# Masked attention joined to the shared-head attention three steps sooner

## Chip, cores, metric

One core of one Trainium2 chip. The metric is device microseconds for one execution of the whole program. The core has five engines with an instruction stream each: TensorE (PE; its weight loads are listed as PEld), VectorE (DVE), ScalarE (ACT), GpSimd (POOL) and SyncE (SP, which issues transfers only). Each works through its own stream in order, and they meet at semaphores.

## What is computed

Two decoder layers on x of shape (32, 128, 128): 32 batches of 128 tokens with 128 features. Layer 0 is self attention, cross attention and a mixture of experts, layer 1 is what the change touches:

```
x = x + L1_attn(layernorm(x))                  # "shared1": 16 heads of 64, averaged in groups of
                                               # four to 4 heads; scores + relative bias, softmax
x = x + L1_xattn(layernorm(x), ctx, ctx, mask) # "cross1": 16 heads of 8, keys and values from ctx,
                                               # energy = where(mask == 0, -1e10, q k / sqrt(8))
x = x + L1_ffn(layernorm(x))                   # mixture of 8 experts and a shared one
```

## The kernel before, in words

**Stages.** The program is written as two functions of engine streams, one after the other: `early` (both attentions and experts of layer 0) and `late` (layer 1). Every attention is a software pipeline. A step `k` on an engine emits the work of several batches at once, each at another point of its way; a batch is 128 tokens, a group is G = 2 batches, so that work on groups is done in every second step.

**The lead.** The shared-head attention of layer 1 is called the lead (`shared_heads`). Its steps run from -7 to 33. Steps -7 to 13 are emitted by the experts stage of layer 0. In step k PE emits (L1257 ff.): the four transposes of the probabilities of batch k (L1265), the eight score products of batch k + 3 (L1275, while k is at most 28), in even steps up to 24 the "front" of a group (transposes of the normalised x, L1283, and after the value products of batch k, L1293, the q and k projections, L1300), in odd steps up to 29 the v projection of a group (L1306), and last the output product of batch k (L1312). The output of batch 31 is in step 31. DVE does per step the reciprocal and the probabilities (L1188, L1191), bias and maximum of the next scores (L1197, L1199), the copy of the value product out of PSUM (L1203), the residual sum (L1209) and the statistics (L309, L289). ACT copies transposes, projections and values out of PSUM and makes the exponentials (L1231 to L1253).

**The masked attention.** The cross attention of layer 1 (`cross1`, function `head_attention` with a mask) has steps k from -11 (FIRST) on. In odd steps from -11 DVE normalises a group (L306, tile `cross_xn`); in even steps from -10 PE transposes it (L996) and ACT copies it out (L869, `xnT_ready`); in odd steps from -9 PE projects q and k (L1010, L1011) and ACT adds the biases (L877, L878), after which POOL splits the result into three bf16 parts (L679 to L685), stores them to DRAM (L689) and adds an output bias to x (L703); SP places them back in another layout (L620). In even steps from -6 PE projects v (L1021). From step -3 the scores of a first pass are formed, in four units a step, each a mask product (L955) and four products of heads (L965), and DVE takes the maxima (L769). From step 0 the second pass comes to it (L958, L969, exponentials on ACT), from step 1 the products with the values (L987). So steps -3 to -1 are "maxima only", and steps from 1 on are full.

**Joining.** `joined_steps` (L153 ff.) writes the order. Before, lead steps 14 to 21 are one turn of a hardware loop, 22 to 24 are emitted alone, and from step `join` = 2 * NG - 2 * FG - 1 = 25 to the lead's last, 33, every lead step is followed by one step of the masked attention, -11 to -3; after that the masked attention goes on alone from step -2. Every engine but SP has this order. At `join` (DVE three steps ahead of it) an engine also waits for `handed`, which says that the early half is over on all engines.

**Banks.** All six PSUM tiles of the masked attention are given to the lead too (call of `make_lead`, L434). The two that matter here: the lead writes its k projection and early transposes to `ps_xv` (its name there is `ps_k`), and its q projection to `ps_qk` (`ps_q`). `take_banks` (L928 ff.) is called by PE at the start of each masked step and waits there until the lead is done with a bank. In step FIRST it waits for `lead.qk_ready` = 2 * NG = 32: all 16 groups' q and k are copied out, of which the last are made in lead step 24.

**Masks.** In lead step `join` - 3 DVE prepares the masks (`read_masks`, L732 to L736); in masked step FIRST PE counts over them into `ps_xv` (`count_masks`, L926), and DVE makes the products' operands from it (`make_drops`, L740 to L745). PE waits for these in step FIRST + 1.

Of the kernel before, what the change touches and what calls it, by code (L numbers as in the profile page):

```python
# [24 lines left out]
B, S, D = 32, 128, 128  # L25
H, HD = 16, 8
G = 2
NG = B // G
# [12 lines left out]
FA, SA, LA, MA, VA = 5, 4, 3, 3, 3  # L41
# [97 lines left out]
def steps(engine, emit, first, loops, last):  # L139

    k = first
    for loop_from, loop_to in loops:
        for k in range(k, loop_from):
            emit(At(None, k))
        with engine.Fori(0, (loop_to - loop_from) // At.STEPS) as i:
            for k in range(loop_from, loop_from + At.STEPS):
                emit(At(i, k))
        k = loop_to
    for k in range(k, last + 1):
        emit(At(None, k))  # L150


def joined_steps(engine, lead, lead_emit, emit, first, loops, last, handed=None, ask=0):  # L153

    def lead_step(t):
        if handed is not None and t.reg is None and t.k == lead.join - ask:
            engine.wait_ge(handed, 1)
        lead_emit(t)

    if lead is None:  # L160
        steps(engine, emit, first, loops, last)
        return
    steps(engine, lead_step, lead.begun, lead.loops, lead.join - 1)
    offset = lead.join - first
    for k in range(lead.join, lead.last + 1):
        lead_step(At(None, k))
        emit(At(None, k - offset))
    steps(engine, emit, lead.last + 1 - offset, loops, last)
# [235 lines left out]
def head_attention(nc, sem, name, x_sb, norm, ident, identb, QK, layers, mask, scale, prepare, opening, make_lead, staging, make_follow, handed):  # L404
# [14 lines left out]
    with ExitStack() as ctx:  # L419
# [14 lines left out]
        lead = None if make_lead is None else make_lead(tiles, ps_max, ps_exp, ps_pv, ps_out, ps_xv, ps_qk)  # L434
# [41 lines left out]
        moments_ready, var_ready, rstd_ready = sem("moments_ready"), sem("var_ready"), sem("rstd_ready")  # L476
# [6 lines left out]
        xnT_ready = sem("xnT_ready")  # L483
        kv_loaded = [sem(f"kv_loaded{p}") for p in range(RING)]
        qk_made = sem("qk_made")
        qk_ready = sem("qk_ready")
        v_made = sem("v_made")
        v_ready = sem("v_ready")
# [16 lines left out]
        o_ready = sem("o_ready")  # L505
# [4 lines left out]
        x_done = sem("x_done")  # L510
# [5 lines left out]
        FIRST, LAST = -2 * FA - 1, NB_ALL + 2  # L516
        LOOPS = [(i * B + 4, i * B + (20 if NL > 1 else 12)) for i in range(NL)]
# [402 lines left out]
        def pe_program(pe):  # L920
# [7 lines left out]
            def take_banks(t):  # L928

                if t.k == FIRST:  # L930
                    pe.wait_ge(lead.qk_ready, 2 * NG)
                if t.k == -MA:
                    pe.wait_ge(lead.biased, B)
                if t.k == 0:
                    pe.wait_ge(lead.pT_ready, B)
                    pe.wait_ge(lead.v_ready, NG)
                if t.k == 1:
                    pe.wait_ge(lead.o_ready, B)
                    pe.wait_ge(lead.x_done, B)
# [111 lines left out]
            def emit(t):  # L1051
# [3 lines left out]
                if lead is not None and t.reg is None:  # L1055
                    take_banks(t)
# [25 lines left out]
                if t.reg is None:  # L1082
# [2 lines left out]
                        pe.wait_ge(v_ready, NG_ALL)  # L1085
                    for j in FRONTS.get(t.k, ()):
                        follow.pe_front(pe, Turn(None, j))
            joined_steps(pe, lead, lead and lead.pe, emit, FIRST, LOOPS, LAST, handed)
            follow.pe(pe)

        return Program(sp_program, pool_program, dve_program, act_program, pe_program)


# [30 lines left out]
def shared_heads(nc, sem, name, x_sb, norm, ident, folded, bias, ctx, bank_scores, bank_pT_v, bank_o, bank_xy, bank_k, bank_q):  # L1124
# [26 lines left out]
    moments_ready, var_ready, rstd_ready, turns_pool = sem("moments_ready"), sem("var_ready"), sem("rstd_ready"), sem("turns_pool")  # L1151
    xn_ready, xT_made, xT_ready = sem("xn_ready"), sem("xT_made"), sem("xT_ready")
    qk_made, qk_ready, v_made, v_ready = sem("qk_made"), sem("qk_ready"), sem("v_made"), sem("v_ready")
    scored, biased, max_ready, exp_done = sem("scored"), sem("biased"), sem("max_ready"), sem("exp_done")
    recip_ready, probs_ready = sem("recip_ready"), sem("probs_ready")
    pT_made, pT_ready = sem("pT_made"), sem("pT_ready")
    pv_done, o_ready, y_made, x_done = sem("pv_done"), sem("o_ready"), sem("y_made"), sem("x_done")
    stats_taken, turns_dve = sem("stats_taken"), sem("turns_dve")
    FG, AHEAD, BEGUN = 3, 3, 14
    FIRST, LAST, LOOPS = -2 * FG - 1, B + 1, [(BEGUN, BEGUN + At.STEPS)]  # L1160

    def par(t, off=0):
        return ((t.k + off) // G) % RING
# [91 lines left out]
    pe = nc.tensor  # L1255
# [81 lines left out]
                last = nc.tensor.matmul(ps_k[:, j, :], (wq, wk)[part - 1][:, j * 128:(j + 1) * 128], xnT[front][:], start=True, stop=True)  # L1337
            last.then_inc(qk_made, 1)

    return Lead(pool_step, dve_step, act_step, pe_step, act_early, pe_early, FIRST, LOOPS, LAST, 2 * NG - 2 * FG - 1, BEGUN, rstd_ready, qk_ready, biased, pT_ready, v_ready, o_ready, x_done)  # L1340


MG = 4
# [1182 lines left out]
def decoder(nc, a, out):  # L2526
    scale = HD ** -0.5
    with ExitStack() as ctx:
# [55 lines left out]
        with ExitStack() as shared:  # L2584
            folded = [sb(shared, f"shared1_{c}", [D, FEAT]) for c in "qkvo"]
            with ExitStack() as first:
                made = matrices(first, 0)
                small = router_tiles(first, 0)
                with ExitStack() as staging:
                    by_rel = sb(staging, "by_rel", [D, RELS])  # L2590
                    by_rel_dram = nc.dram_tensor("by_rel_dram", (KVH, S, RELS), F32)
                    to_split = splits(staging, 0, made)
                    halves = sb(staging, "halves", [D, 2, FEAT])

                    folds = [(sb(staging, f"shared1_{c}_whole", [D, REP, FEAT]), a[f"shared1_{c}"], halves, total, factor)
                             for c, total, factor in zip("qkvo", folded, (1.0, 1.0 / REP, 1.0 / REP, 1.0))]
                    opening = Opening(nc, first_sems.stage("load"), staging, a, x_sb, norm, ident, identb, by_rel)
                    early = heads(first_sems.stage("heads0"), "heads0", (("self0", None), ("cross0", a["ctxT"])), None,
                          Prepare(to_split, folds, (by_rel, by_rel_dram, bias)), opening, None, staging,
                          mixture(first_sems.stage("experts0"), 0, small, made))  # L2600
                used = first_sems.runs(first_sems.made)
            with ExitStack() as second:
                made = matrices(second, 1)
                small = router_tiles(second, 1)
                with ExitStack() as staging:
                    shared_sem = sems.stage("shared1")

                    def lead(stack, *banks):
                        ahead.lead = shared_heads(nc, shared_sem, "shared1", x_sb, norm, ident, folded, bias, stack, *banks)
                        first_sems.release()  # L2610
                        return ahead.lead
                    late = heads(sems.stage("cross1"), "cross1", (("cross1", a["ctxT"]),), (a["mask"], a["maskT"]), Prepare(splits(staging, 1, made)), None,
                          lead, staging, mixture(sems.stage("experts1"), 1, small, made))
# [131 lines left out]
```

## Time and profile before

| | |
|---|---|
| median of 3 runs | 1152.3 us |
| lowest and highest | 1145.33 and 1161.37 us |
| profiled execution, its own time | 1154.38 us |
| its span, first to last instruction | 1152.6 us |
| mean granted TensorE clock, share of full speed | 0.949 |
| PE busy, share of the span | 89% |
| DVE busy, share of the span | 78% |

Times in the text are microseconds from the start of the span of the profiled execution. A line of a timeline gives the start, the duration, the engine, the source line, the operation, output and inputs, the number of instructions merged, and in brackets the idle time ahead of it and what ended it. A line of a table of stretches gives start and end, length, then for PE, PEld, DVE, ACT and POOL the busy time and the number of instructions, then the granted clock of TensorE, the busy share of the DMA engines and the GB/s. A granted clock of 1.00 is 2.4 GHz, one of 0.50 is 1.2 GHz.

### The profile page before, as it was taken

How to read it: one execution, taken by the hardware profiler on the slowest of the kernel's cores; microseconds unless marked ns; L12 is line 12 of the kernel's file. 1: busy time of each engine (PE TensorE's matmuls, PEld its weight loads, DVE VectorE, ACT ScalarE, POOL GpSimd, SP SyncE). 2: the span in 40 equal slices, each digit the busy share in tenths (PEclk: the TensorE clock that was granted, in tenths of full speed). 3: DMA queues.
4: the chain of work that ended last, by engine and by line, in shares of the span. 5: the costliest groups of instructions: out<-in, count | busy, mean ns of one | idle time of the engine just before them, and what ended most of it. 6: DMA issues, size and time to landing. Idle time of an engine off the chain costs nothing.

```text
span 1152.6 us, 33382 instructions
## 1 busy us (share of the span) xinstructions
PE 1021.9 (89%) x10238; PEld 706.9 (61%) x10238; DVE 902.4 (78%) x2462; ACT 677.5 (59%) x1737; POOL 628.8 (55%) x956
## 2 busy tenths in 40 slices
PE   3799999889998979999987778879999999878997
PEld 2466666556656768777665556664555555655775
DVE  5588899788888588888997887745777777758896
ACT  1277777667777444555445656642666666545774
POOL 8667778766775376603346443166566651424553
PEclk9999999899989589999999999976999999879999
DMA  5765577866675011323321001025545640044450
GB/s 143 175 145 126 124 153 164 159 139 134 131 182 158 6 48 66 120 79 95 88 77 44 20 20 54 1 60 121 112 106 115 121 105 19 6 174 168 183 183 28
DMA packets 81442, 119.66 MB, mean 104 GB/s; under 512 B 16704, under 2 KB 62688, under 8 KB 80272
## 3 DMA queue, kind: packets, MB, share of 16 engines
q1 hardware_dynamic: 66688, 85.24, 31.3%
q0 software_dynamic: 9472, 27.27, 7.9%
q10 hardware_dynamic: 5136, 5.31, 2.3%
q8 instruction: 78, 1.28, 0.5%
q14 instruction: 68, 0.56, 0.2%
HBM read 80.75 MB, written 36.18 MB: 101 GB/s over the span
## 4 chain that ended last, share of the span: by engine, by line
PE 50%; DVE 25%; issue 13%; DMA 4%; POOL 4%; ACT 2%; DVEq 1%; SPq 1%; POOLq 0%; ACTq 0%
PE heads_ps_pv L987 4%; PE heads_ps_max L965 4%; DVE heads_neg_max L769 4%; PE cross_ps_max L965 4%; PE cross_ps_pv L987 3%; PE cross_ps_max L955 3%; PE experts_ps_gu L2453 3%; PE cross_ps_exp L958 2%; DVE experts_hidden L1739 2%; PE cross_ps_out L1312 2%; PE heads_ps_out L1049 2%; DMA QK<-heads_qk_parts 2%; DVE x_sb L2306 2%; PE experts_ps_gu L2455 2%; PE experts_ps_gu L2454 2%
## 5 line engine op out<-in xcount | busy, mean ns | idle before, releaser
L769 DVE TENSOR_REDUCE heads_neg_max<-heads_ps_max 128x4 f32<-128x512 f32 x256 | 169.0, 680 | 38.0 <-PE heads_ps_max L965 36.3
L843 ACT ACTIVATE heads_E<-heads_ps_exp 128x512 f32<-128x512 f32 x256 | 150.3, 603 | 23.2 <-PE heads_ps_pv L987 16.9
L769 DVE TENSOR_REDUCE cross_neg_max<-cross_ps_max 128x4 f32<-128x512 f32 x128 | 86.8, 685 | 48.6 <-PE cross_ps_max L965 48.1
L965 PE MATMUL heads_ps_max<-QK 48*128 48x128 bf16 x1024 | 104.2, 227 | 9.9 <-DMA QK<-heads_qk_parts 6.2
L2158 POOL DMA_INDIRECT experts_gathered<-experts_y_dram,experts_index x64 | 62.1, 970 | 79.3 <-DMA experts_y_dram<-experts_y_sb 44.9
L969 PE MATMUL heads_ps_exp<-QK 50*128 50x128 bf16 x1024 | 104.3, 224 | 0.0
L843 ACT ACTIVATE cross_E<-cross_ps_exp 128x512 f32<-128x512 f32 x128 | 76.6, 599 | 39.0 <-PE cross_ps_exp L969 20.5
L2381 ACT ACTIVATE experts_act_out<-experts_ps_gu 128x256 f32<-128x256 f32 x110 | 42.3, 384 | 92.1 <-PE experts_ps_gu L2455 91.9
L965 PEld LDWEIGHTS heads_ps_max<-QK 48*128 48x128 bf16 x1024 | 59.4, 97 | 52.5 <-issue 20.0
L987 PE MATMUL heads_ps_pv<-heads_E,heads_V 128*32 128x128 f32 x2048 | 86.1, 287 | 0.9 <-issue 0.9
L1598 POOL TENSOR_TENSOR experts_hidden_lo<-experts_hidden,experts_hidden_hi 128x512 fp32r<-128x512 f32 x32 | 46.9, 1466 | 70.2 <-ACT experts_hidden_hi L1825 70.2
L1739 DVE TENSOR_TENSOR experts_hidden<-experts_act_out,experts_share 128x512 f32<-128x512 f32 x64 | 67.2, 1060 | 15.9 <-issue 6.3
L2143 POOL DMA_INDIRECT experts_xs_dram<-QK,experts_index x64 | 61.5, 960 | 33.4 <-DMA experts_xs_dram<-QK,experts_index 23.0
L2474 PE MATMUL experts_ps_y<-experts_down,experts_hT_hi 128*128 (+1 forms) x220 | 67.6, 328 | 7.9 <-DVE experts_hT_lo L2278 5.8
L1825 ACT CAST experts_hidden_hi<-experts_hidden 128x512 fp32r<-128x512 f32 x72 | 44.7, 621 | 44.2 <-DVE experts_hidden L1739 32.4
L1242 ACT ACTIVATE shared_E<-shared_scores,shared_neg_max 128x128 f32<-128x128 f32 x128 | 49.8, 390 | 30.7 <-DVE shared_probs L1191 30.7
L965 PEld LDWEIGHTS cross_ps_max<-QK 48*128 48x128 bf16 x512 | 29.9, 97 | 56.2 <-issue 56.2
L2273 DVE TENSOR_TENSOR experts_hidden<-experts_act_out,experts_ps_gu 128x256 f32<-128x256 f32 x110 | 45.8, 417 | 20.1 <-ACT experts_act_out L2381 17.5
L969 PEld LDWEIGHTS heads_ps_exp<-QK 50*128 50x128 bf16 x1024 | 59.0, 96 | 1.8 <-issue 1.0
L296 POOL TENSOR_TENSOR norm_var_eps<-norm_moments,norm_eps 128x2 f32<-128x2 f32 x64 | 14.7, 229 | 82.4 <-DVE norm_moments L289 82.3
L987 PEld LDWEIGHTS heads_ps_pv<-heads_E,heads_V 128*32 128x32 f32 x2048 | 50.2, 112 | 15.3 <-issue 2.1
L2475 PE MATMUL experts_ps_y<-experts_down,experts_hT_lo 128*128 (+1 forms) x220 | 57.8, 284 | 0.0
(323 smaller groups left out, 3238.7 us busy)
## 6 DMA issues: line engine op xcount, KB each, us to landing
experts_share<-experts_cT_dram SPq DMA_DIRECT2D x7, 2304.0 KB, 8.7
heads_qk_parts<-heads_parts POOLq DMA_DIRECT2D x32, 384.0 KB, 4.4
QK<-heads_qk_parts SPq DMA_DIRECT2D x64, 192.0 KB
QK<-heads_qk_parts SPq DMA_DIRECT2D x64, 128.0 KB
cross_qk_parts<-cross_parts POOLq DMA_DIRECT2D x16, 384.0 KB, 4.2
QK<-cross_qk_parts SPq DMA_DIRECT2D x32, 192.0 KB
experts_xs_dram<-load_stats SPq DMA_DIRECT2D x26, 192.0 KB, 3.1
experts_xs<-experts_xs_dram SPq DMA_DIRECT2D x78, 64.0 KB, 2.1
```

Of the source, the lines that this page charges most:

```text
L769: nc.vector.tensor_reduce(neg_max[:, half, heads.start:heads.stop], ps_max[:, u % 2, :].rearrange("q (h k) -> q h k", h=HU), AX.X, ALU.max ...
L843: nc.scalar.activation(E[:, half, heads.start:heads.stop, :], ps_exp[:, u % 2, :].rearrange("k (h q) -> k h q", h=HU), ACT.Exp, scale=scal ...
L965: last_max = nc.tensor.matmul(ps_max[:, u % 2, i * S:(i + 1) * S], QK[q_of][rows, 0, h, max_of], QK[q_of][rows, 1, h, max_of], start=not m ...
L969: last_exp = nc.tensor.matmul(ps_exp[:, u % 2, i * S:(i + 1) * S], QK[e_of][rows, 1, h, exp_of], QK[e_of][rows, 0, h, exp_of], start=not m ...
L987: last = nc.tensor.matmul(ps_pv[TILE * i:TILE * (i + 1), u // 2 * S:(u // 2 + 1) * S], V[p][:, j, window:window + TILE], E[:, half, h, :], ...
L1242: last = nc.scalar.activation(E[:, s, :], scores[t.k % 2][:, s // 2, s % 2, :], ACT.Exp, bias=neg_max[t.k % 2][:, s:s + 1], accum_out=sums ...
L1598: nc.gpsimd.tensor_tensor(hidden_lo[b][:], hidden[b][:], hidden_hi[b][:].bitcast(F32), ALU.subtract).then_inc(lo_pool, 1)
L1739: nc.vector.tensor_tensor(as_group(hidden[b][:]), as_group(act_out[b][:]), share[t.k % 2][:, row, :, :], ALU.mult).then_inc(hidden_ready, 1)
L2143: pool.indirect_dma_start(xs_dram[h], bass.IndirectOffsetOnAxis(index[:, choice, b:b + 1], 0), xn[b // MG][:, b % MG, :], None).then_inc(s ...
L2158: pool.indirect_dma_start(gathered[n % GATHERS][:], None, y_dram[h], bass.IndirectOffsetOnAxis(index[:, choice, b:b + 1], 0)).then_inc(loa ...
L2474: nc.tensor.matmul(out, hT_hi[u % 3][:, these], both, start=c == 0, stop=False, skip_group_check=True)
L2475: last = nc.tensor.matmul(out, hT_lo[u % 3][:, these], both, start=False, stop=c == 1, skip_group_check=True)
```

## The change

`join` goes from 2 * NG - 2 * FG - 1 to 2 * NG - 2 * FG - 4, from 25 to 22. Lead steps 22 to 33 are followed by masked steps -11 to 0, and the masked attention is alone from step 1. Two fronts of the lead, in its steps 22 and 24, now lie beside masked steps that use the same two banks. So the wait in `take_banks` is cut in two: step FIRST needs only 30 of the lead's 32 (groups up to step 22), step 1 - 2 * FA = -9 needs all; and PE waits in lead step `join` + 2 = 24 until the first transposed group of the masked attention has been copied out of `ps_xv`. The lead's loop over steps 14 to 21 is gone: the same steps are written out.

```diff
@@ -928,6 +928,8 @@
             def take_banks(t):
 
                 if t.k == FIRST:
+                    pe.wait_ge(lead.qk_ready, 2 * NG - 2)
+                if t.k == 1 - 2 * FA:
                     pe.wait_ge(lead.qk_ready, 2 * NG)
                 if t.k == -MA:
                     pe.wait_ge(lead.biased, B)
@@ -1085,7 +1087,12 @@
                         pe.wait_ge(v_ready, NG_ALL)
                     for j in FRONTS.get(t.k, ()):
                         follow.pe_front(pe, Turn(None, j))
-            joined_steps(pe, lead, lead and lead.pe, emit, FIRST, LOOPS, LAST, handed)
+
+            def lead_emit(t):
+                if t.reg is None and t.k == lead.join + 2:
+                    pe.wait_ge(xnT_ready, 1)
+                lead.pe(t)
+            joined_steps(pe, lead, lead_emit, emit, FIRST, LOOPS, LAST, handed)
             follow.pe(pe)
 
         return Program(sp_program, pool_program, dve_program, act_program, pe_program)
@@ -1157,7 +1164,7 @@
     FG, AHEAD, BEGUN = 3, 3, 14
-    FIRST, LAST, LOOPS = -2 * FG - 1, B + 1, [(BEGUN, BEGUN + At.STEPS)]
+    FIRST, LAST, LOOPS = -2 * FG - 1, B + 1, []
@@ -1337,7 +1344,7 @@
-    return Lead(pool_step, dve_step, act_step, pe_step, act_early, pe_early, FIRST, LOOPS, LAST, 2 * NG - 2 * FG - 1, BEGUN, rstd_ready, qk_ready, biased, pT_ready, v_ready, o_ready, x_done)
+    return Lead(pool_step, dve_step, act_step, pe_step, act_early, pe_early, FIRST, LOOPS, LAST, 2 * NG - 2 * FG - 4, BEGUN, rstd_ready, qk_ready, biased, pT_ready, v_ready, o_ready, x_done)
```

## Rows read from the trace of the kernel before

**Rows 1.** The page: busy time, share and instructions of each engine.
```profile
span 1152.6 us, 33382 instructions
PE 1021.9 (89%) x10238; PEld 706.9 (61%) x10238; DVE 902.4 (78%) x2462; ACT 677.5 (59%) x1737; POOL 628.8 (55%) x956
```
**Rows 2.** Stretches from lead output to lead output, then by masked step.
```profile
717.29:725.94 8.65, 7.93 (x63) 6.12 (x63) 6.49 (x19) 6.25 (x24) 1.46 (x3) 1.00 0.00 0
...
735.00:743.46 8.46, 7.93 (x63) 6.11 (x63) 6.47 (x18) 6.26 (x24) 1.44 (x3) 1.00 0.00 0
743.46:748.90 5.44, 2.68 (x26) 2.08 (x27) 4.46 (x13) 2.70 (x11) 0.00 (x0) 0.90 0.01 3
748.90:755.03 6.13, 6.13 (x30) 5.02 (x31) 3.20 (x9) 2.64 (x11) 0.99 (x3) 0.53 0.00 1
755.03:759.45 4.42, 3.22 (x29) 2.46 (x27) 3.40 (x9) 3.43 (x12) 2.11 (x3) 1.00 0.00 0
759.45:763.05 3.60, 2.92 (x22) 2.41 (x23) 2.01 (x7) 2.09 (x9) 3.09 (x7) 1.00 0.02 5
763.05:767.11 4.06, 2.57 (x21) 1.93 (x19) 2.93 (x7) 2.33 (x8) 3.74 (x6) 1.00 0.32 97
767.11:772.97 5.86, 4.10 (x23) 3.09 (x23) 1.16 (x5) 1.33 (x3) 5.01 (x10) 0.60 0.73 127
772.97:778.10 5.13, 4.37 (x14) 3.43 (x15) 1.44 (x7) 1.10 (x3) 4.18 (x8) 0.50 0.49 112
778.10:784.33 6.23, 6.23 (x25) 2.90 (x24) 2.08 (x3) 1.21 (x3) 5.39 (x11) 0.50 0.83 146
784.33:791.16 6.83, 6.13 (x29) 3.16 (x28) 5.06 (x10) 0.63 (x2) 5.96 (x12) 0.50 0.50 119
791.16:797.60 6.44, 6.44 (x26) 3.00 (x25) 2.25 (x4) 1.46 (x4) 1.89 (x3) 0.50 0.63 142
797.60:803.77 6.17, 6.16 (x62) 2.72 (x65) 5.06 (x11) 3.16 (x7) 5.17 (x10) 0.89 0.23 54
...
822.05:834.39 12.34, 12.34 (x170) 7.16 (x174) 9.19 (x26) 7.55 (x18) 7.51 (x15) 1.00 0.51 113
```
**Rows 3.** Timeline of PE around the joint: outputs, projections, transposes.
```profile
730.45 0.61 PE L1312 MATMUL cross_ps_out<-shared_o,shared_oT 128*128 128x128 f32 x4
...
739.52 0.61 PE L1312 MATMUL cross_ps_out<-shared_o,shared_oT 128*128 128x128 f32 x4
...
748.90 1.22 PE L1312 MATMUL cross_ps_out<-shared_o,shared_oT 128*128 128x128 f32 x4 [2.74 <-DVE shared_oT L1203]
...
755.48 0.60 PE L1010 MATMUL cross_ps_qk<-cross_xnT,cross_wq 128*128 128x256 f32 x2
755.91 0.59 PE L1011 MATMUL cross_ps_qk<-cross_kvT,cross_wk 128*128 128x256 f32 x2
...
768.60 1.19 PE L1021 MATMUL cross_ps_xv<-cross_wv,cross_kvT 128*128 128x128 f32 x4 [0.55 <-ACT cross_xnT L869]
```
**Rows 4.** Timeline of DVE: mask preparation, mask operands, normalising, maxima.
```profile
731.93 0.23 DVE L734 TENSOR_SCALAR cross_keep<-cross_mask_in 128x256 f32<-128x256 int32 x1
...
744.62 0.28 DVE L740 TENSOR_SCALAR cross_any_all<-cross_ps_xv 128x128 f32<-128x128 f32 x1
...
745.78 0.60 DVE L306 TENSOR_SCALAR cross_xn<-x_sb,norm_mean,norm_rstd 128x128 f32<-128x128 f32 x2
...
779.31 0.69 DVE L769 TENSOR_REDUCE cross_neg_max<-cross_ps_max 128x4 f32<-128x512 f32 x1 [3.60 <-PE cross_ps_max L965]
```
**Rows 5.** Timeline of ACT: the lead's last k copy.
```profile
739.72 0.58 ACT L1249 COPY shared_K<-cross_ps_xv 128x512 f32<-128x512 f32 x1
```
**Rows 6.** Timeline of POOL: first split, its store, second split.
```profile
757.16 1.17 POOL L679 TENSOR_TENSOR cross_qm<-cross_qk_full,cross_any_all 128x256 f32<-128x256 f32 x1 [5.08 <-ACT cross_qk_full L877]
...
763.92 0.97 POOL L689 DMA_DIRECT2D cross_qk_parts<-cross_parts  x1 [0.29 <-POOL cross_parts L685]
...
767.11 0.72 POOL L679 TENSOR_TENSOR cross_qm<-cross_qk_full,cross_any_all 128x256 f32<-128x256 f32 x1
```

## Prediction

> **What bounds the kernel now.** I read the page first: PE is busy for 89% of 1152.6 us, DVE for 78% [rows 1]. These shares say little about one joint between two stages, so I then cut the trace at the lead's output products (L1312), one per lead step, and behind the last of them at the starts of the masked steps [rows 2]. The reader is to see four regimes there.
>
> Lead alone: two steps take 8.46 us, of which PE is busy 7.93 us, at clock 1.00. The first of the two, the even one with the front, is filled by PE (output to output 735.00 to 739.52, 4.52 us); the second, 3.94 us, waits for DVE, whose chain ends in the copy for the output.
>
> Lead with masked steps -11 to -7, lead steps 25 to 29: 5.44, 6.13, 4.42, 3.60, 4.06 us. The second of these is long because the clock fell to 0.53, after PE had waited 2.74 us for DVE [rows 3]; the mask operands and a normalisation had been put into DVE's stream just before [rows 4].
>
> From 767 us on: the steps get thin, the clock falls again, to 0.60 in the stretch from 767.11, and then stays at 0.50 up to 797.60. Masked steps -3, -2 and -1 (maxima only) take 6.23, 6.83 and 6.44 us there, with PE busy nearly all of the time: work that is small at 2.4 GHz and PE-bound at 1.2 GHz. Step 0 takes 6.17 us at 0.89.
>
> Full masked steps: two take 12.34 us, PE busy throughout [rows 2]. A full step costs 6.17 us wherever it lies, and the change leaves their number and content alone. So the whole effect is on the time from the output of lead step 22 (730.45) [rows 3] to the start of masked step 1 (803.77) [rows 2]: 73.3 us. If masked step 1 starts g earlier, the program ends g earlier.
>
> **What the change does to this stretch.** Its work is the same; its overlap differs. Before, three lead steps (22 to 24) stand alone and masked steps -2, -1, 0 stand alone. After, there is no step alone. I go from output to output.
>
> Up to lead output 30. DVE's mask operands are four instructions of 0.28 us, L740 to L745 (one shown), and the normalisation 0.60 us [rows 4]; before they made the step 25 to 26 5.44 us instead of 3.94, that is +1.5. They now fall between 22 and 23: 3.94 + 1.5 = 5.4.
>
> Step 23 to 24 is PE-bound, 4.52 us. Two transposes of the masked attention come in, and then the **added wait**: PE stands at the head of lead step 24 until ACT has copied them. Behind it on PE are all of lead step 24 and thereby DVE's copy and sum of that step. The nearest row for such a wait is PE's before the v projection at 768.60, 0.55 us, on the same copy of ACT [rows 3]. Bounds: 0, if ACT's copy is covered by the tail of the transposes, and 1.5 us, if ACT is still at the exponentials of a step that DVE has delayed by that 1.5. I take 0.5, nearest to the row. 4.5 + 0.3 + 0.5 = 5.3.
>
> Step 24 to 25: masked step -9 must wait for the **lead's last k copy**, the moved half of the old wait. In the trace this copy starts at 739.72, 0.20 after the output of its step, and takes 0.58 [rows 5]; the output itself is 0.45 before PE is free, so some 0.4 is left. Then q and k projections, 755.48 to 756.35, 0.87 us at full clock [rows 3]. PE had about 0.5 idle here. 3.94 + 0.4 + 0.9 - 0.5 = 4.7. Bounds: 3.94 and 5.7.
>
> 25 to 26: two transposes, in DVE's shadow: 3.9. 26 to 27 has projections and a lead v projection, and looks like the measured 4.42 of 27 to 28 [rows 2]: 4.5. 27 to 28 gets transposes, the 0.55 wait and a v projection (0.6 at full clock) on a DVE-bound step: 4.0. 28 to 29: before 3.60, transposes out, 0.87 in: 4.2. 29 to 30: before 4.06, 0.87 out, 1.4 in: 4.5.
>
> Sum: 5.4 + 5.3 + 4.7 + 3.9 + 4.5 + 4.0 + 4.2 + 4.5 = 36.5 us. Before it was 767.11 - 730.45 = 36.7. So the lead isn't delayed to speak of: three more masked steps begun, at no cost, mostly because the idle time of DVE-bound lead steps takes them, and because the slow 6.13 goes.
>
> From lead output 30 on the clock decides. **Low clock**, as in the trace of before: 30 to 31 took 5.86, with masked step -6 in it (transposes, wait, v projection: 2.1 at this clock); with step -3 in its place, 5.9 - 2.1 + 6.2 = 10.0. Then lead output 31 (0.9) and step -2, 6.8: 7.7. Steps -1 and 0 as before, 6.4 and 6.2. Sum 30.3, and 73.3 - 36.5 - 30.3 = **6.5 us gained**.
>
> **The loop written out.** A pair in the loop takes 8.65 us, one outside 8.46 [rows 2]: 0.2 for each of four pairs, 0.8 at most; lost is at most the same, if code that isn't a loop were slower to arrive, which the pairs outside don't show. I take 0.5 gained. The mask preparation (0.23 for L734, three such, [rows 4]) moves from lead step 22 to 19: nothing.
>
> **What the earlier steps pull with them.** DVE's normalisation in masked step 1 needs the statistics of all lead batches; these come through POOL's lead step 33, behind POOL's split of step -1. POOL's first split starts at 757.16 and the second at 767.11, 10 us for a group with everything [rows 6]; projections now come every 8.2 to 9 us, so POOL drifts later by a few us, but the first store was issued at 763.92 and its group first used at 778.10, 14 us later [rows 2, 6], and after the change six steps still lie between projection and use. Bounds: 0 and 3 us. I take 0. SP's placements follow the stores and aren't moved past anything. The bank waits of steps -3 and 0 are for lead steps 28 and 31, which are over.
>
> Together 7 us. The profiled execution took 1154.4 (its span 1152.6 and 1.8 around it), 2.1 above the median of the runs; against the median: 1152.3 - 7 = **1145.3**, say 1145.
>
> **The rivals.**
>
> *Full clock (A).* If the denser steps keep the clock up, -3 to -1 are bound by DVE: four maxima of 0.69 [rows 4], small ones and in odd steps a normalisation, 3.6 to 4.2 us each. Then 30 to 31: 3.3 + 3.6 = 6.9; to the start of -1: 4.7; -1: 4.2; 0: 5.9. Sum 21.7 in place of 30.3, the gain is 15.5, the time 1137. For it: lead steps 26 to 29 now have PE busy 3 to 4 us each. Against it: in steps 30 and 31 PE has still only lead transposes, value products and output beside the maxima, and from 778.10 to 797.60 PE was busy 18.8 of 19.5 us with maxima and projections and the clock stayed at 0.50 [rows 2].
>
> The Trainium skill, "TensorE: Matmul & The Clock Gate", Part 1, holds that throttled is the default state and that sustained matmul activity releases it. By that rule these steps would have been fast already in the kernel before. The measurement decides against it here.
>
> *Nothing moved (B).* The work added to lead steps is paid for one by one: each of the eight outputs up to 30 comes 0.8 later than I have it, because DVE, ACT and PE wait for each other in turn. Then 36.5 becomes 43, the gain is 0 to 2, the time 1151. For it: lead pairs had only 0.5 us of PE idle in 8.46 [rows 2]. Against it: from lead step 25 on the fronts are gone and PE's idle time is 0.7 to 2.8 a step.
>
> *Slower (C).* The clock falls while PE waits for DVE between 22 and 23, as it did after the 2.74 us wait [rows 3], and stays low, as from 767 us on. Now lead step 24 with its front lies in it. PE's work per step from 24 to 27 at full clock is about 4.7, 4.1, 2.6, 4.1; doubled 31 us, where I have 18.4: 12.8 lost, 7 gained, the time 1158. At this rate (12.8 lost in 31 us) it decides from about 17 us of low clock on. For it: the same DVE work sits in front. Against it: the wait is shorter (the v projection of lead step 23 lies in it), and the first drop ended within the 6.13 us step, under just such lead work [rows 2]. If it ends as soon here, it costs 3 us and stays inside my forecast.
>
> *The change doesn't do what it says (D):* if masked step 1 then waits for POOL or QK, the three steps are gained and stood out again: as B, 1151; counted there.
>
> **How the numbers follow.** My case 0.55, A 0.2, B (with D) 0.15, C 0.1. My own case reaches from 3 to 10 us gained, 1142 to 1149. The range takes in A, with the spread of the runs before (7 us to either side of their median), and nearly C: 1134 to 1156. About 2% (23 us) is what a measurement of this kernel can tell from no change. No case reaches it; 0.03 for faster, where A meets an early run, 0.02 for slower, C with a lost clock further on, and 0.95 within.
>
> **What would show it.** Right: lead output 30 about 36 us after output 22; masked step 1 about 66 us after output 22; the wait before lead step 24 about 0.5 us; maxima-only steps of 6.2 to 6.8 us at clock 0.50; 12.34 us per two full steps as before. Wrong: maxima-only steps near 4 us at 1.00 (A); lead steps 23 to 30 over 5 us each at 1.00 (B); a clock of 0.50 over lead steps 24 to 27 (C); PE idle on a transfer or DVE on the statistics about masked step 1 (D).

## The result, and the profile after

| | before | after |
|---|---|---|
| median of 20 runs | 1152.05 us | 1141.99 us |
| lowest, highest | 1141.28, 1171.29 | 1134.86, 1162.9 |
| ratio after to before | | 0.9944, 95% interval 0.9921 to 0.9967 |
| span of the profiled execution | 1152.6 us | 1139.4 us |

The ratio stands for 6.5 us (3.8 to 9.1 by its interval), where 7 was forecast. It is taken over those runs of each kernel that lie within 1.5% of its fastest, which is why the two medians of all runs are 10.1 us apart, and the profiled executions of E7 and E11 below are not among such runs. The single profiled executions differ by 13.2 us, so the first question is which of these belong to the change. The page after:

```profile
span 1139.4 us, 33355 instructions
PE 1004.7 (88%) x10238; PEld 694.0 (61%) x10238; DVE 901.8 (79%) x2462; ACT 677.8 (59%) x1737; POOL 629.0 (55%) x956
```

The same number of PE instructions as in [rows 1], with 17 us less of busy time: not less work but a higher clock over it. Both traces, cut at 300 us (only what follows is shown), at a point shortly ahead of the lead's first output, at lead output 22, at the first mask product of masked step 1, 197.15 us behind that, and at the end. The stretch from lead output 22 to masked step 1 is called the joint. First the kernel before, then the one after (length, then busy times of PE, PEld, DVE, ACT, POOL, granted clock, DMA share, GB/s):

```profile
300.00:615.00 315.00, 289.24 (x2349) 221.20 (x2346) 263.99 (x867) 169.04 (x466) 156.65 (x197) 0.93 0.34 93
615.00:730.45 115.45, 95.89 (x720) 71.74 (x717) 92.49 (x267) 73.73 (x262) 48.46 (x73) 0.99 0.11 31
730.45:802.85 72.40, 61.38 (x377) 40.35 (x376) 42.69 (x113) 30.64 (x100) 39.42 (x71) 0.74 0.30 62
802.85:1000.00 197.15, 193.67 (x2583) 113.73 (x2580) 145.22 (x386) 122.41 (x288) 104.24 (x184) 1.00 0.42 89
1000.00:1152.60 152.60, 126.97 (x512) 94.00 (x512) 115.98 (x162) 90.39 (x161) 63.71 (x45) 0.93 0.39 140
```

```profile
300.00:611.60 311.60, 281.23 (x2387) 214.96 (x2387) 264.75 (x877) 170.04 (x471) 158.85 (x200) 0.96 0.34 94
611.60:725.55 113.95, 94.92 (x725) 70.94 (x725) 92.97 (x268) 74.05 (x263) 47.95 (x73) 1.00 0.12 31
725.55:791.45 65.90, 54.71 (x377) 35.38 (x376) 41.68 (x110) 30.80 (x100) 39.11 (x69) 0.87 0.33 71
791.45:988.60 197.15, 193.68 (x2583) 113.78 (x2580) 144.52 (x386) 122.45 (x288) 104.94 (x186) 1.00 0.42 88
988.60:1139.40 150.80, 125.08 (x512) 92.54 (x512) 115.94 (x162) 90.39 (x161) 63.67 (x45) 0.94 0.40 141
```

3.4 us lie ahead of anything that was edited and 1.8 us behind it, both where the granted clock differs. They are put down to chance of single executions: E0 below, the same kernel as after, spans 1144.7 us. 1.5 us lie in the lead up to output 22, of which 0.8 are the loop (four pairs of steps at 8.46 in place of 8.65) and the rest again clock. **6.5 us lie at the joint**, 72.40 to 65.90. The full masked steps take as long as before. The fifth stretch was cut to one length in both, so its length says nothing; but the same product near its end stands 195.28 us behind masked step 1 in both (PE, before and after):

```profile
998.13 0.96 PE L1871 MATMUL experts_ps_tok<-experts_router,QK 128*128 128x16 f32 x8
...
986.73 0.96 PE L1878 MATMUL experts_ps_tok<-experts_router,QK 128*128 128x16 f32 x8
```

The prediction ended the joint 0.9 later, at the first product with the values (803.77 in its text, 803.70 in the timeline; 792.30 after); on that cut it is 73.3 to 66.8 us, and 66.8 was forecast (36.5 + 30.3). From here on the end is the first mask product of masked step 1. The joint after, cut as in [rows 2], from lead output 22 to 31 and then by masked step:

```profile
725.55:731.21 5.66, 3.90 (x31) 2.73 (x29) 4.81 (x16) 2.85 (x12) 1.11 (x3) 1.00 0.00 1
731.21:736.63 5.42, 4.95 (x36) 3.89 (x37) 3.34 (x9) 3.77 (x14) 0.00 (x0) 1.00 0.01 3
736.63:741.62 4.99, 4.39 (x33) 3.29 (x32) 3.62 (x11) 3.54 (x13) 2.19 (x3) 1.00 0.00 0
741.62:745.66 4.04, 2.61 (x28) 2.01 (x27) 3.11 (x7) 3.16 (x11) 3.53 (x7) 1.00 0.00 0
745.66:750.62 4.96, 4.38 (x32) 3.24 (x32) 4.06 (x11) 2.96 (x13) 4.46 (x9) 1.00 0.33 95
750.62:756.09 5.47, 3.36 (x31) 2.55 (x31) 2.88 (x7) 3.46 (x13) 4.66 (x8) 1.00 0.82 145
756.09:760.62 4.53, 3.56 (x24) 2.90 (x25) 2.43 (x9) 2.95 (x12) 3.89 (x8) 1.00 0.44 106
760.62:764.92 4.30, 2.64 (x24) 1.92 (x22) 1.68 (x5) 1.95 (x5) 3.74 (x7) 1.00 0.83 146
764.92:772.00 7.08, 5.46 (x41) 3.23 (x41) 5.05 (x13) 1.42 (x3) 4.85 (x9) 1.00 0.40 96
772.00:779.02 7.02, 7.02 (x31) 3.94 (x32) 3.43 (x7) 0.63 (x2) 5.37 (x11) 0.51 0.27 61
779.02:785.47 6.45, 6.45 (x27) 3.00 (x25) 2.70 (x7) 1.47 (x4) 0.32 (x2) 0.50 0.59 137
785.47:791.45 5.98, 5.98 (x49) 2.67 (x49) 4.57 (x9) 2.66 (x6) 4.99 (x10) 0.69 0.23 52
```

Two things are to be seen. Output 22 to 30 takes 39.4 us, where 36.5 was forecast and 36.7 was before: the eight lead steps do pay for their company. And the clock is 1.00 down to 772 us, through masked step -3, and low (1.2 GHz) for 17 us only, where before it was low for 7 us beside the lead and for 31 us from 1.2 us behind output 30 on. Output 30 to masked step 1 takes 27.4 us on the prediction's cut (26.5 on this one), where 30.3 was forecast. Two errors of 2.9 us stand against each other.

### The profile page after: what moved, and what is told of

It reads as the page before. It is cut to its first block, busy times and chain, and to the rows that moved or that the text cites. A ratio compares the mean times of both kernels' runs of the same rounds, so it can differ in the third digit from the quotient of the medians.

```text
span 1139.4 us, 33355 instructions
## 1 busy us (share of the span) xinstructions
PE 1004.7 (88%) x10238; PEld 694.0 (61%) x10238; DVE 901.8 (79%) x2462; ACT 677.8 (59%) x1737; POOL 629.0 (55%) x956
## 4 chain that ended last, share of the span: by engine, by line
PE 48%; DVE 25%; issue 13%; DMA 5%; POOL 4%; ACT 3%; SPq 1%; DVEq 1%; POOLq 0%; ACTq 0%
PE heads_ps_max L967 4%; PE heads_ps_pv L989 4%; PE cross_ps_max L967 4%; DVE heads_neg_max L769 3%; PE cross_ps_pv L989 3%; DMA QK<-heads_qk_parts 3%; PE cross_ps_max L957 3%; PE experts_ps_gu L2460 3%; PE cross_ps_exp L960 2%; DVE experts_hidden L1746 2%; PE cross_ps_out L1319 2%; DVE x_sb L2313 2%; PE experts_ps_gu L2462 2%; PE experts_ps_gu L2461 2%; PE heads_ps_out L1051 2%
## 5 line engine op out<-in xcount | busy, mean ns | idle before, releaser
L843 ACT ACTIVATE cross_E<-cross_ps_exp 128x512 f32<-128x512 f32 x128 | 76.6, 599 | 39.4 <-PE cross_ps_exp L971 21.2
L967 PE MATMUL cross_ps_max<-QK 48*128 48x128 bf16 x512 | 52.6, 226 | 0.0
```

The costliest lines, as they stand in the source:

```text
L843: nc.scalar.activation(E[:, half, heads.start:heads.stop, :], ps_exp[:, u % 2, :].rearrange("k (h q) -> k h q", h=HU), ACT.Exp, scale=scal ...
L967: last_max = nc.tensor.matmul(ps_max[:, u % 2, i * S:(i + 1) * S], QK[q_of][rows, 0, h, max_of], QK[q_of][rows, 1, h, max_of], start=not m ...
```

## The experiments

E1 to E4 and E11 ran on a chip on which the kernel before takes 1224.8 and 1223.2 us, the others on two like the first (1150.6 and 1147.2). What makes that chip slower lies in other stages: in E11 lead output 22 comes at 798.91 us in place of 730.45, while the joint of this kernel has the same length on both. Each joint length below is read from one profiled execution, each ratio from several runs of both kernels (E2: only 4 runs of its own).

**E1, the loop alone.**

```diff
 (kernel before)
-    FIRST, LAST, LOOPS = -2 * FG - 1, B + 1, [(BEGUN, BEGUN + At.STEPS)]
+    FIRST, LAST, LOOPS = -2 * FG - 1, B + 1, []
```

> The kernel before with only the lead's loop over steps 14 to 21 written out, joined at 25 as before. Theory (the gain is overlap at the joint; the loop is worth little): lead odd steps 14 to 21 fall from 4.13 to 3.94 us, 0.8 us in all, output 22 to the start of masked step 1 stays at about 73 us, and the time is within 0.1% of before. Rival (the written-out loop is what gained): 5 to 7 us less than before, ratio about 0.995, most of it ahead of lead step 22.

Measured: ratio 1.0017 (0.9973 to 1.006). Odd lead steps 14 to 21 take 3.95 us instead of 4.14, 0.8 in all; the joint takes 72.39 us, as before (72.40). The loop isn't the gain.

**E2, E3, E4, joined at 24, 23 and 21.** E2 needs neither new wait. E3 and E4 move them to where these orders need them (of E4 the waits in PE's lead steps are shown, not those that move in `take_banks`):

```diff
 (E2: kernel before, LOOPS = [])
-    ... B + 1, LAST, 2 * NG - 2 * FG - 1, BEGUN
+    ... B + 1, LAST, 2 * NG - 2 * FG - 2, BEGUN
 (E4: kernel of the change)
-    ... 2 * NG - 2 * FG - 4, BEGUN
+    ... 2 * NG - 2 * FG - 5, BEGUN
+                if t.reg is None and t.k == lead.join + 1:
+                    pe.wait_ge(mask_step, 5)
+                if t.reg is None and t.k == lead.join + 3:
+                    pe.wait_ge(xnT_ready, 1)
+                    pe.wait_ge(qk_ready, 2)
```

> Joined at 24, one step sooner, with no use of a bank in turns: all fronts of the lead are over when the masked attention begins; the loop is written out. Theory (each step of earlier joining saves a masked step that would stand alone and costs 1 to 1.5 us of lead time): output 22 to masked step 1 about 71 us in place of 73.3, the time about 3 us under before (2.2 and the loop's 0.8). Rival (the gain is the clock: fewer long waits and a later, shorter low stretch, and it appears whenever the phase of the clock allows): no relation to the number of steps; 66 or 73 us.

> Joined at 23, two steps sooner: lead step 24 with its front waits for the mask count's reader in place of the transposed group's copy. Theory: output 22 to masked step 1 about 69 us, the time about 5 us under before. Rival: as for one step, no relation to the number of steps.

> Joined at 21, four steps sooner, lead steps 22 and 24 both take turns on the banks. Theory: one more step overlapped, masked step 0 beside lead step 32, output 21 to masked step 1 about 68 us (70 in the kernel of the change with its 65.9 from output 22), the time about 2 us under the kernel of the change, 8 to 9 under before. Rival (the handoffs and POOL's 9 to 10 us per group take over): masked step 1 no earlier than in the kernel of the change, PE idle before masked step 1 or 3 on a placement of q and k, time as the kernel of the change or slower.

Measured, with before and the change beside them; times in us. The first length begins at lead output 14, because the mask preparation moves across output 22; in the rows of 25 and 24 a low stretch of 3.4 us lies between outputs 14 and 22, and E1, without it and without the loop, has 106.3 us there in place of 107.6.

| joined at | output 14 to masked step 1 | output 22 to masked step 1 | low clock in the joint | ratio to before |
|---|---|---|---|---|
| 25 (before) | 107.6 | 72.4 | 37.5 | 1 |
| 24 (E2) | 95.0 | 60.4 | 0 | 0.9846 (0.977 to 0.9921) |
| 23 (E3) | 97.4 | 62.9 | 6.8 | 0.9955 (0.9918 to 0.9993) |
| 22 (change) | 99.8 | 65.9 | 17.1 | 0.9944 (0.9921 to 0.9967) |
| 21 (E4) | 102.3 | 66.8 | 23.9 | 0.992 (0.9886 to 0.9955) |

This does not fit the theory of the prediction. One step sooner shortens the joint by 12 us (71 us was expected, 66 or 73 by the rival), and each further step lengthens it (E3: 69 expected; E4: 68 from output 21 expected, 72.3 measured; masked step 1 came no earlier than in the change, as the rival had it, but PE nowhere waited for a placement of q and k). The lengths follow the time at 1.2 GHz. The ratios are too coarse to follow: E4's is below the change's, though its joint is 0.9 longer. In E2 the maxima-only steps -3 to -1 and step 0 run at 2.4 GHz, as rival A had it:

```profile
830.19:834.36 4.17, 2.67 (x20) 2.04 (x21) 2.06 (x7) 1.32 (x3) 3.76 (x8) 1.00 0.77 179
834.36:836.30 1.94, 1.48 (x10) 1.23 (x11) 0.93 (x5) 0.37 (x1) 1.69 (x4) 1.00 0.08 23
836.30:840.04 3.74, 3.60 (x26) 1.86 (x24) 2.03 (x3) 0.81 (x3) 3.10 (x6) 1.00 0.93 165
840.04:844.47 4.43, 3.71 (x30) 2.10 (x28) 4.04 (x9) 1.03 (x4) 4.14 (x9) 1.00 0.63 152
844.47:848.72 4.25, 3.77 (x28) 1.95 (x25) 3.09 (x6) 1.07 (x4) 2.98 (x6) 1.00 0.57 112
848.72:855.01 6.29, 4.84 (x49) 2.19 (x48) 5.45 (x11) 3.68 (x9) 5.57 (x10) 1.00 0.71 138
```

The first line is lead output 30 to 31, the second the rest up to masked step -3, then the steps -3 to 0: 3.74, 4.43, 4.25, 6.29, against 6.23, 6.83, 6.44 [rows 2] and, for step 0 on this cut, before:

```profile
797.60:802.85 5.25, 5.24 (x49) 2.33 (x49) 4.47 (x9) 2.60 (x6) 4.56 (x9) 0.87 0.11 23
```

**E0, the change again.**

> The kernel of the change again, beside the others on one chip. Theory (overlap): output 22 to masked step 1 between 62 and 68 us, whatever the clock does, and the time 6 to 8 us under before. Rival (it was the clock's chance that its profile had only 17 us at 1.2 GHz about the joint): a stretch of 70 us or more if the low stretch is 30 us again.

Measured: ratio 0.9929 (0.9886 to 0.9972). The joint took 65.90 us with 17.1 us low from lead output 31 on, to the tenth the same as in the first profile. As the clock repeated too, this doesn't decide between the theory and its rival.

**E5 and E9, the added wait moved** from the head of lead step 24 to just ahead of the k projection, the first product that writes the bank:

```diff
             for weight, dst in ((wq, ps_q), (wk, ps_k)):
+                if dst is ps_k and before_k is not None:
+                    before_k()              # pe.wait_ge(xnT_ready, 1), in lead step join + 2
```

> The kernel of the change with the added wait of lead step 24 moved from the head of the step to just before the k projection, the first product that writes the bank. Theory (the wait costs its 0.46 us of PE at the head because everything of step 24 is behind it): step 23 to 24 from 5.42 to 4.95 us, no idle time before the k projection, the time 0.5 us less, too little to measure. Rival (the wait is covered by DVE anyway): 5.4 stays, the idle time shows up before the output of step 24.

> A second look at the kernel with the late wait, to see whether the clock's course at the joint repeats. If it repeats: 3.4 us at 1.2 GHz in step 26 to 27 and none after output 30, 61.0 us from output 22 to masked step 1. If it is chance: a low stretch of 17 us or more after output 30, 65 to 66 us.

The wait as the change has it, and the two others about it (timeline of PE after):

```profile
726.39 0.49 PE L926 MATMUL cross_ps_xv<-cross_keep,cross_ones 128*128 128x128 f32 x2 [0.23 <-ACT shared_K L1256]
...
732.61 0.66 PE L1272 MATMUL cross_ps_exp<-ident,shared_probs 128*128 128x128 f32 x4 [0.46 <-ACT cross_xnT L869]
...
737.47 0.70 PE L1012 MATMUL cross_ps_qk<-cross_xnT,cross_wq 128*128 128x256 f32 x2 [0.23 <-ACT shared_K L1256]
```

With the late wait, step 23 to 24 takes 4.73 us (E9: 4.74) in place of 5.42, PE busy throughout. So the wait at the head cost 0.69 us, 0.46 of standing, and PE's busy time fell by 0.22 as well (4.95 to 4.73); 4.95 us was expected. E5's ratio is 0.9928 (0.9888 to 0.9968), not to be told from E0; E9 is a single run (1144.12 us) and has none. The clock in the joint did not repeat: E5 has 3.4 us low, beside the lead, and a joint of 60.97, E9 6.8 + 10.2 us low and 65.90. E5 from output 30 to masked step -2, then steps -2, -1 and 0:

```profile
772.40:780.03 7.63, 6.02 (x44) 3.77 (x45) 5.05 (x13) 1.43 (x3) 5.32 (x10) 1.00 0.34 84
780.03:783.58 3.55, 3.55 (x29) 1.98 (x27) 2.96 (x6) 0.63 (x2) 2.38 (x5) 1.00 0.01 2
783.58:788.17 4.59, 3.83 (x27) 1.95 (x24) 3.48 (x9) 1.06 (x4) 2.60 (x5) 1.00 0.94 192
788.17:793.40 5.23, 4.68 (x49) 2.19 (x48) 4.45 (x9) 3.13 (x8) 4.40 (x8) 1.00 0.55 123
```

These two executions of one kernel give the price of the low clock by itself: 13.6 us more at 1.2 GHz lengthen the joint by 4.9 us, 0.36 us for each. What one costs will depend on the steps that it falls on.

**E6, E10 and E8, fillers.** E6 is the change, E10 the change with the late wait, E8 the kernel before, each with products whose result nobody uses:

```diff
+    def fill(t, n):                                # lead: ahead of the waits for pT and o
+        if t.reg is None and t.k >= 31:            # E8: 30
+            pe.wait_ge(v_ready, NG)
+            for _ in range(n):
+                nc.tensor.matmul(ps_v[:, 0, 0:S], ident[:], ident[:], start=True, stop=True)
+                    if masked and t.reg is None and -MA <= t.k < 0:      # ahead of each unit
+                        pe.wait_ge(lead.v_ready, NG)
+                        for _ in range(2):                               # E8, E10: 1
+                            nc.tensor.matmul(ps_exp[:, 1, 0:S], ident[:], ident[:], ...)
```

> The kernel of the change with filler products (f32, 128 columns, result unused, into a part of a PSUM bank that nobody reads then): two before each unit of masked steps -3 to -1, and two before the value products and the output of lead step 31. Theory (the clock falls there because PE works too little, and half clock is what makes steps -2 to 0 long): the clock stays at 1.00 from output 30 to masked step 1, steps -2 and -1 take 4.5 to 5.5 us each in place of 7.0 and 6.45, output 30 to masked step 1 about 23 us in place of 26.5, the time 3 us less. Rival (fillers are only more work, or the clock falls anyway): the clock is 0.50 over -2 and -1, each takes 10 to 11 us, the time 6 to 8 us more.

> The kernel of the change with the late wait and fewer fillers: one before each unit of masked steps -3 to -1, one before the value products and one before the output of lead step 31. New theory (clock): the clock stays up, and the fillers cost half as much as before: output 30 to masked step 1 about 23 us, output 22 to masked step 1 about 62, the time 2 us under the kernel of the change. Rival (one filler is too little): the clock falls after output 30 as in the change, 27 us or more from there to masked step 1.

> The kernel before, joined at 25, with filler products alone (f32, 128 columns, result unused): two before the value products and two before the output of lead steps 30 and 31, one before each unit of masked steps -3 to -1. New theory (clock): if these keep the clock at 1.00 from output 30 on, the stretch from output 22 to masked step 1 falls from 72.4 to about 63 us without any earlier joining, and the time is 5 us or more under before. Rival (overlap, the theory of the prediction): at full clock too the kernel before is longer than the change by two steps alone, 70 us or more. If the clock falls in spite of the fillers, steps -3 to -1 take 7 to 8.5 us each and the run tells nothing of the two.

E6, output 22 to 30 and to masked step -2, then steps -2, -1, 0:

```profile
734.09:773.46 39.37, 29.78 (x233) 22.52 (x232) 25.94 (x74) 24.64 (x85) 23.58 (x40) 1.00 0.31 63
773.46:783.20 9.74, 9.44 (x73) 7.09 (x73) 5.53 (x15) 1.43 (x3) 6.06 (x12) 1.00 0.26 59
783.20:788.71 5.51, 5.51 (x45) 3.76 (x43) 3.17 (x7) 0.87 (x3) 4.11 (x8) 1.00 0.36 82
788.71:793.92 5.21, 5.21 (x39) 3.36 (x37) 2.72 (x8) 1.22 (x4) 0.36 (x2) 1.00 0.63 163
793.92:799.17 5.25, 4.75 (x49) 2.18 (x48) 4.47 (x9) 2.65 (x6) 4.56 (x9) 1.00 0.25 54
```

The clock stays up and the steps are shorter, as the clock theory says, but the fillers are work of their own (output 30 to 31 8.74 in place of 7.08), and 25.7 us from output 30 to masked step 1, where 23 was expected, is only 0.8 under the change. Ratio 0.9933 (0.9897 to 0.9968), as E0. E10: no low clock behind output 30, 23.45 us from there, 63.8 in all, with a low stretch of 3.4 us beside the lead. E5 is the same kernel without fillers and had the same clock: 21.00 us from output 30, so E10's fillers cost 2.45. E10's ratio of 0.998 (0.9945 to 1.0014) shows no gain.

E8 went half as expected. Behind output 30 the clock stayed at 1.00 to the end of step -4, masked step -3 then waited 1.17 us for the placement of its q and k, and 0.8 us behind this wait the clock fell for 6.8 us (3.4 us more were low beside the lead):

```profile
776.66 0.39 PE L959 MATMUL cross_ps_max<-cross_drop_q,identb 128*128 128x512 bf16 x1 [1.17 <-DMA QK<-cross_qk_parts]
```

68.5 us for the joint, 3.9 under before and not 9; ratio 0.9996 (0.9963 to 1.0028), where 5 us less was expected. With the steps ahead of it at full clock, a transfer that the slow steps had hidden came to light; and these fillers alone don't do what the change does. As the clock fell after all, E8 doesn't decide between clock and overlap.

**E7, joined at 24 again, and E11, the kernel before against itself.**

> The kernel joined at 24 once more (its first runs were few, and on another chip). New theory (what the change gained is mostly that less of the joint runs at 1.2 GHz; overlap by itself is worth about 0.6 us per step of earlier joining): output 22 to masked step 1 is 60 to 61 us when the clock stays up, 70 or more when it falls for 30 us after output 30. If the clock stays up here as it did before, the length is a property of the order of the work and not of one execution, and the time is 10 to 12 us under before. Rival (the clock at the joint differs from execution to execution for one and the same kernel): another length in this profile, and a time like that of the change, 6 to 8 us under before.

> The kernel before against itself: a third look at its joint and a measure of the noise. If the long low stretch belongs to the order of its work: 30 us at 1.2 GHz from just before lead output 31, output 22 to masked step 1 72.4 us again. If it is chance: another length, as low as 62 us, where all of the joint runs at 2.4 GHz. The ratio is 1 within 0.3%.

E7: ratio 0.9914 (0.9876 to 0.9951), 9.9 us. The joint took 62.41 us, with 10.2 us low from within masked step -2 on: neither 60 nor 70. So the course of the clock can vary for one kernel, here in both traces with less low clock than before. Against E2 10.2 us more at 1.2 GHz cost 2.1 us, 0.20 for each. E11: 72.50 us with 6.8 us and 30.7 us low, the third trace of the joint of before (72.40, 72.39 in E1) and the third on the same course. But the ratio of the kernel to itself came out at 0.9951 (0.9909 to 0.9993): an interval here can miss 1 by chance, and half a per cent from one such comparison is not proof. No ratio here is as far as 2% from 1. That the change gains 6 us rests on two comparisons (0.9944, 0.9929) and on the traces: 65.90 us in both of the change, 72.39 to 72.50 in three of before.

## Why the prediction was right, point by point

**The total: right, in good part by luck.** 7 was forecast, 6.5 measured, and the joint came to the forecast 66.8 us because an error of +2.9 us and one of -2.9 us cancelled. The median, 1142.0 where 1145 was forecast, lies at the edge of the prediction's own case (1142 to 1149).

**The place: right.** Nothing but the joint and the loop moved. Full masked steps are unchanged.

**The loop: right at its upper bound.** 0.8 us, measured alone in E1.

**Steps 22 to 25: right.** 5.4, 5.3, 4.7 forecast; 5.66, 5.42, 4.99 measured. The added wait was put at 0.5, by the row of a like wait, and stood for 0.46, though it cost 0.69 (E5, E9). A wait of 0.23 of the mask count on the lead's k copy was overlooked.

**Steps 26 to 30: 2 us too low**, most of it in one term, 27 to 28: 4.0 forecast, 5.47 measured. I had set PE's additions against DVE's chain and taken the longer of the two. They add up. PE stood 0.55 us for ACT's copy and did the v projection before the lead's transposes; DVE could not write the next probabilities until those were done, and then PE waited for DVE's whole chain (DVE and PE after):

```profile
753.69 0.69 DVE L1198 TENSOR_TENSOR shared_probs<-shared_E,shared_recip 128x512 f32<-128x512 f32 x1 [1.75 <-PE cross_ps_exp L1272]
...
756.09 0.71 PE L1319 MATMUL cross_ps_out<-shared_o,shared_oT 128*128 128x128 f32 x4 [1.53 <-DVE shared_oT L1210]
```

So idle time of PE in this ring of waits was no room for work ahead of the ring's next link. Rival B had this mechanism, and overrated it (6.5 us, measured 2.9 over all eight steps).

**Output 30 to masked step 1: 2.9 us too high** (30.3 forecast, 27.4 measured on that cut). The failed step is "Low clock, as in the trace of before", carried over to -3, -2, -1 as if it belonged to these steps. Masked step -3 ran at 1.00: output 30 to 31 took 7.08, rival A's 6.9 and not my 10.0. Output 31 with step -2 took 7.0 at 0.51 (7.7 forecast), step -1 6.45 at 0.50 (6.4 forecast), and step 0 6.8 on that cut (6.2). So my case and rival A each hold for a part.

**The cause of the gain: not as forecast.** The sum gave the 6.5 us to overlap, with the low clock behind output 30 left as it was. What the change would bring at like clock no trace shows, as before was never seen at full clock; it can be estimated:

- Before, from its joint of 72.4. At 1.00 E2's steps -3 to 0 take 18.7 us, before 24.75. The fallen lead step of before takes 6.13, E2's like one 4.60. Output 30 to 31 takes 5.86, at full clock about 4.3 (E2's 4.17 has somewhat less in it). The rest up to step -3 takes 5.13, about 3.7 at full clock. That makes 62 us, and 63 if the wait of 1.17 us that E8 showed comes to it.
- After: 60.4, that is the change with E5's steps (from the first mask product of step -3 on 20.45 us, lead output 31 among them, in place of 25.98).
- E2 measured 60.4 at full clock.

So joining three steps sooner is worth about 1.5 to 2.5 us at a fixed clock, nothing of it beyond the first step, and the other 4 to 5 of the 6.5 us come from 20.4 us less at 1.2 GHz. The second way to the same share needs no such estimate of before: at the 0.36 us (E5, E9) and 0.20 us (E2, E7) that one kernel paid for each us at 1.2 GHz, 20.4 us are 4.1 to 7.4. Both say that more than half of the gain is clock; the exact share is not shown. E2 against the change shows the order: two steps *less* of early joining, 3.5 to 5.5 us shorter, and at least no slower in time (0.9846 and 0.9914 against 0.9944 and 0.9929; the intervals overlap, so that E2 is the better kernel is likely, not shown).

**Slips in the working.** Rival C's doubled 31 us less 18.4 are 12.6, not 12.8. Rival B's counter says that PE idles 0.7 to 2.8 us in every step from 25 on, but in the step of 6.13 us it was busy throughout [rows 2]. Neither changes a case.

**Rival C** did not come: after the 1.5 us of DVE-bound waiting before output 23 the clock stayed at 1.00. **Rival D** came only in E8, 1.17 us.

**What stays open.** Why the order joined at 25 falls to 1.2 GHz between lead outputs 30 and 31 in all three traces, and that joined at 24 in neither of two. The steps concerned differ in which lead step stands beside a projection, since 24 and 25 differ in parity, but E3 has the parity of 25 and stayed up there. It wasn't tried to change the parity alone. In E8, with fillers in lead steps 30 and 31, this fall did not come, so thin work on PE there may be a part of it; that is one trace, and the clock of one kernel varies.

## What to carry to other kernels

The joint of two pipelined stages was thin on PE here, and how much of it ran at the low clock outweighed what was overlapped: try each offset, and read the granted clock of every one, more than once, before crediting a gain to overlap. Two executions of one kernel with different clocks give the price of the low clock without any model. If a new wait guards a buffer, put it at the first instruction that writes the buffer (0.69 us here). When adding work to steps that are bound by a ring of engines, ask for each piece whether it stands ahead of a link of the ring; if so it adds, however idle its engine is.

## What the runs showed of the hardware that was not expected

The clock can fall without a long wait of PE ahead of it. In E9 PE was busy 3.55 of 3.55 us in masked step -2, at 1.00, and the clock fell 2.5 us into the next step, in which PE had by then stood for 0.58 and 0.18 us. In E7 it fell 3.5 us into step -2, in which PE had stood for 0.71 and 0.16 us, behind a step -3 with 3.60 of 3.74 us busy. E9, steps -2 and -1:

```profile
776.24:779.79 3.55, 3.55 (x30) 1.98 (x27) 2.97 (x6) 0.63 (x2) 2.38 (x5) 1.00 0.01 2
779.79:786.04 6.25, 5.49 (x28) 2.74 (x25) 3.47 (x9) 1.47 (x4) 2.85 (x6) 0.70 0.94 205
```

Once the clock was low, PE being busy did not bring it back at once. Before, it was at 0.50 over all three maxima-only steps, with PE busy 18.8 of 19.5 us; after, over steps -2 and -1, with PE busy throughout. It rose only in step 0, where the second pass of scores joins, but not at once with it: 1.4 us into the step before, 3.7 after, 6.5 in E9.

The Trainium skill, "TensorE: Matmul & The Clock Gate", Part 1, has sustained matmul activity release the throttle. The stretches just named, with PE busy nearly all the time at the low clock, do not agree with that for this mix of bf16 head products on 48 rows, mask products and one f32 projection a step. With two f32 filler products ahead of each unit (E6) the clock never fell in the joint; with one (E8) it did, behind the wait of 1.17 us, and with one in E10 it did not behind output 30.
